# A decoder layer on one core: the down-projection summed over two pairs of weight blocks, five shared PSUM banks, weight tiles prepared one at a time

## What is computed

```python
x = x + mamba_and_mlp(layernorm(x))           # MLP: 2048 hidden columns, float32 weights
x = x + smooth_quant_experts(layernorm(x))    # one small expert for each of the 4 sequences
x = x + ffn(layernorm(x))                     # FFN: 4096 hidden columns, 4-bit weights
...
hn = _rmsnorm(h, rms2_w)                      # h: the residual after the Mamba block
mlp = jax.nn.silu(hn @ gate_w.T) * (hn @ up_w.T) @ down_w.T
return res + mlp
...
Wg = dequant_nvfp4(gate_W_packed, gate_scales)     # code -> value, times a scale per 32 columns
gate = jnp.einsum('th,nh->tn', xt, Wg)
up = jnp.einsum('th,nh->tn', xt, Wu)
gelu = jnp.tanh(0.7978845608028654 * (gate + 0.044715 * gate ** 3)) * gate * 0.5 + gate * 0.5
out = jnp.einsum('tn,hn->th', gelu * up, Wd)
```

## Time and profile before

| | |
|---|---|
| median of 3 runs | 3127.9 us (3126.78 to 3128.18) |
| the profiled execution | 3122.57 us, span of its instructions 3120.8 us |
| PE busy | 2763.6 us (89%) |
| DVE busy | 2285.1 us (73%) |
| ACT busy | 1158.0 us (37%) |
| POOL busy | 1099.5 us (35%) |
| weight stage (first gate matmul to last add) | 1268.5 to 3115.9 us |
| DMA | 275.37 MB, mean 88 GB/s |

### The profile page before, as it was taken

One profiled execution on the slowest core, in us unless ns is written; L12 is line 12 of the kernel. 1 busy time (PEld: TensorE's weight loads), 2 busy tenths in 40 slices (PEclk: granted clock), 3 DMA queues, 4 the chain that ended last, 5 costly groups with the idle time before them and its releaser, 6 DMA issues.

```text
span 3120.8 us, 32784 instructions
## 1 busy us (share of the span) xinstructions
PE 2763.6 (89%) x11248; PEld 1932.1 (62%) x11248; DVE 2285.1 (73%) x2903; ACT 1158.0 (37%) x1668; POOL 1099.5 (35%) x776
## 2 busy tenths in 40 slices
PE   6488898888888857999999999899999999999998
PEld 2344444444444235778777777777777777777777
DVE  6599999999999954444476667777776666676664
ACT  3355555555555433332244433332332321222221
POOL 0288888888888811010000001111111111212210
PEclk8798998888889668999999999999999999999999
DMA  3554555456455254011111012112111111111111
GB/s 131 179 171 143 161 150 155 142 158 163 130 171 145 58 212 155 21 68 61 61 41 59 23 41 61 41 41 61 39 39 37 29 56 46 42 41 41 42 55 59
DMA packets 152215, 275.37 MB, mean 88 GB/s; under 512 B 27248, under 2 KB 27760, under 8 KB 151536
## 3 DMA queue, kind: packets, MB, share of 16 engines
q1 hardware_dynamic: 152048, 273.27, 28.6%
HBM read 178.27 MB, written 61.34 MB: 77 GB/s over the span
## 4 chain that ended last, share of the span: by engine, by line
PE 47%; DVE 21%; ACT 10%; SPq 7%; issue 6%; POOL 6%; DMA 3%; DVEq 0%; POOLq 0%; ACTq 0%
PE ps L1508 11%; PE ps L1510 10%; PE ps L1509 10%; PE ps L1548 7%; ACT ps L764 4%; PE ps L1558 4%; DVE state L1165 4%; SPq L603 3%; POOL wdeq L1053 3%; DVE alo L1460 2%; PE ps L1620 2%; POOL read L1019 2%; DVE prod L1454 2%; DVE glo L1228 2%; SPq L607 1%
## 5 line engine op out<-in xcount | busy, mean ns | idle before, releaser
L1053 POOL TENSOR_TENSOR wdeq<-packed,scales 128x1024 f32<-128x1024 f16 x96 | 229.7, 2392 | 1454.4 <-DVE packed L1285 1020.9
L1019 POOL TENSOR_TENSOR read<-state,c_t 128x512 f32<-128x512 f32 x512 | 655.1, 1291 | 141.2 <-DVE state L1165 117.5
L1165 DVE TENSOR_TENSOR_SCAN state<-ps,drive 128x512 f32<-128x512 f32 x512 | 618.3, 1208 | 14.1 <-ACT ps L764 13.1
L1508 PE MATMUL ps<-xh,ghi 128*128 128x512 f32 x1536 | 609.1, 397 | 1.7 <-DVE res L1220 0.9
L1510 PE MATMUL ps<-xh,glo 128*128 128x512 f32 x1536 | 598.4, 390 | 0.0
L1509 PE MATMUL ps<-xl,ghi 128*128 128x512 f32 x1536 | 598.1, 389 | 0.0
L764 ACT ACTIVATE ps<-ps,a_exp 128x512 f32<-128x512 f32 x512 | 338.9, 662 | 468.2 <-PE ps L1548 467.2
L1508 PE MATMUL ps<-ahi,ghi 128*128 128x512 f32 x768 | 323.1, 421 | 93.3 <-DVE res L1439 74.8
L1439 DVE TENSOR_TENSOR res<-res,ps 128x512 f32<-128x512 f32 x384 | 258.7, 684 | 184.5 <-PE ps L1510 183.9
L1156 DVE TENSOR_TENSOR drive<-ps,b_t 128x512 f32<-128x512 f32 x512 | 339.8, 664 | 21.7 <-PE ps L1548 21.1
L1548 PE MATMUL ps<-dpack,sel 128*128 128x512 f32 x512 | 261.0, 510 | 103.9 <-DVE state L1165 102.3
(11 more groups left out here) (167 smaller groups left out, 3709.5 us busy)
## 6 DMA issues: line engine op xcount, KB each, us to landing
whi<-w_d SPq DMA_DIRECT2D x63, 256.0 KB, 3.9
wlo<-w_d SPq DMA_DIRECT2D x63, 256.0 KB, 4.8
x_d<-ev SPq DMA_DIRECT2D x32, 256.0 KB, 3.1
x_t<-x_d SPq DMA_DIRECT2D x32, 256.0 KB, 4.8
b_d<-ev SPq DMA_DIRECT2D x32, 256.0 KB
b_t<-b_d SPq DMA_DIRECT2D x32, 256.0 KB, 4.0
c_d<-ev SPq DMA_DIRECT2D x32, 256.0 KB, 3.0
c_t<-c_d SPq DMA_DIRECT2D x32, 256.0 KB, 3.2
```

The lines of the kernel that those rows point to most:

```text
L1019: pool.tensor_tensor(read[:, n % RRING, :], state[:, n % SRING, :], c_t[:, g % 2, :], ALU.mult).then_inc(read_ready, 1)
L1053: pool.tensor_tensor(wdeq[:, :].rearrange("p (h n) -> p h n", h=2), codes, scale, ALU.mult).then_inc(deq, 1)
L1165: dve.tensor_tensor_scan(state[:, n % SRING, :], ps[:, n % 2, :], drive[:, n % DRING, :], 0.0, ALU.mult, ALU.add)\
L1508: pe.matmul(out_, w_h, x_h, start=(start and k == 0), stop=False)
```

## The change

1. **Two passes become one, of 24 slots (index E).** Slots 0 to 15 make gate and up for eight units (two pairs), slots 16 to 23 make eight down products, one a slot, each summed in PSUM over both pairs: 12 matmuls instead of 6. There are 24 double passes with the same 6912 matmuls, and each residual block is added once in a double pass: 192 adds instead of 384. `ahi` and `alo` have four tiles each instead of two.
2. **Five shared banks.** Every product of the stage, gate, up or down, takes the next of banks 0 to 4 in turn. `bank_taken(V)` waits for the reader of the product five slots before.
3. **Weight tiles one by one.** There is a ring of five places for `ghi`/`glo`. Tile T (six for each double pass) is loaded at slot 4T - 19, unpacked at 4T - 14, its high part made at 4T - 12, its low part at 4T - 11. Raw data have two buffers, each for one tile, loaded by 1 DMA for the MLP, and by 9 for the FFN (1 for codes, 8 for scales), once tile T - 2 has been dequantised or split.
4. `prod` is gone: DVE multiplies in place into `act_o`, and ACT waits for `alo` of the unit before the last before it writes `act_o` again.
5. Ahead of the stage tiles 0 and 1 are prepared where three were, tile 2 five steps of the output projection later, tiles 3 and on inside the loop.

```diff
-    ghi = [[post(f"ghi{s}{w}", [P, 1024], F32R, R1 + 24576 * s + 4096 * w) for w in range(3)]
-           for s in range(2)]
...
-    prod = [post(f"prod{s}", [P, S], F32, R1 + 69632 + 2048 * s) for s in range(2)]
+    ghi = [post(f"ghi{s}", [P, 1024], F32R, R1 + 8192 * s) for s in range(WRING)]
...
+    ahi = [post(f"ahi{j}", [P, 2 * S], F32R, R1 + 40960 + 8192 * j) for j in range(4)]
...
+        def prepared_at(p, off):
+            T, rest = divmod(p + 12 - off, 4)
+            return [T] if rest == 0 and 3 <= T < ALL_T else []
+        def free_bank(V):
+            return V % 5
...
@@ SP @@
-                for w, name in enumerate(("gate", "up", "down")):
-                    sp.dma_start(packed[:, w, :], t[name + "_codes"][q]).then_inc(codes_loaded, 16)
+                if T >= MLP_T + 2:
+                    sp.wait_ge(deq, T - MLP_T - 1)
+                elif T >= 2:
+                    sp.wait_ge(w_lo, T - 1)
...
@@ ACT @@
-                if Q:
-                    act.wait_ge(gate_ready, 4 * (Q - 1) + 1)
+                if E and k == 0:
+                    act.wait_ge(up_ready, 8 * E - 4)
+                if E and k == 1:
+                    act.wait_ge(gate_ready, 8 * E)
+                if E and k == 2:
+                    act.wait_ge(up_ready, 8 * E)
...
+                if E and k in (3, 4):
+                    act.wait_ge(down_ready, 8 * E)
+                if k == 5:
+                    act.wait_ge(gate_ready, 8 * E + 4)
...
                     if U >= 2:
-                        act.wait_ge(prod_done, U - 1)
+                        act.wait_ge(a_lo, U - 1)
...
-                if i in (4, 6, 8) and Q + 1 < ALL_Q:
-                    w_high(Q + 1, i // 2 - 2)
+                for T in prepared_at(p, 0):
+                    w_high(T)
...
@@ DVE @@
-            for p in range(12 * ALL_Q + 1):
...
+            for p in range(24 * ALL_E + 1):
+                E, i = divmod(p, 24)
+                if i == 0 and E:
+                    add_down(E - 1, 7)
...
-                if i in (9, 10, 11):
-                    for k in (2 * i - 18, 2 * i - 17):
-                        add_down(8 * Q + k)
-                if i in (1, 3, 5) and MLP_Q <= Q + 1 < ALL_Q:
-                    unpack(Q + 1, i // 2)
-                if i in (5, 7, 9) and Q + 1 < ALL_Q:
-                    w_low(Q + 1, i // 2 - 2)
+                if i >= 17:
+                    add_down(E, i - 17)
+                for T in prepared_at(p, -2):
+                    if T >= MLP_T:
+                        unpack(T)
+                for T in prepared_at(p, 1):
+                    w_low(T)
...
@@ PE @@
-                        if f == 0:
-                            pe.wait_ge(a_lo, 4 * Q + 3 + bb)
-                        if D_ >= 2:
-                            pe.wait_ge(added, D_ - 1)
+            def bank_taken(V):
+                if V >= 5:
+                    E, i = divmod(V - 5, 24)
+                    if i >= 16:
+                        pe.wait_ge(added, 8 * E + i - 15)
+                    elif i % 2:
+                        pe.wait_ge(prod_done, 8 * E + i // 2 + 1)
+                    else:
+                        pe.wait_ge(act_done, 8 * E + i // 2 + 1)
+                return ps[:, free_bank(V), :]
...
+                    if i == 16:
+                        pe.wait_ge(w_lo, 6 * E + 6)
+                    if f == 0:
+                        pe.wait_ge(a_lo, 8 * E + 7 + bb)
+                    d = [((6 * E + 4 + j // 2) % WRING, D * (j % 2) + P * f) for j in range(4)]
+                    three_pass(bank_taken(p), [
+                        (ghi[s][:, at:at + P], glo[s][:, at:at + P],
+                         ahi[j][:, cols(bb)], alo[j][:, cols(bb)]) for j, (s, at) in enumerate(d)])\
+                        .then_inc(down_ready, 1)
```

More of the change, by code:

```diff
@@ L305, in build @@
         x_added = sem("x_added")
-        w_loaded4 = sem("w_loaded4")
-        codes_loaded = sem("codes_loaded")
+        tile_loaded = [sem(f"tile_loaded{s}") for s in range(2)]
         bits = sem("bits")
@@ L565, in load_chunk, with load_tile @@
                       .then_inc(yz_loaded[m % CHUNKS], 16)
[L567 to L572 removed]
+            def load_tile(T):
+                Q, w = tile_of(T)
+                ffn, h, q = stage(Q)
+                if T >= MLP_T + 2:
+                    sp.wait_ge(deq, T - MLP_T - 1)
+                elif T >= 2:
+                    sp.wait_ge(w_lo, T - 1)
+                if not ffn:
+                    sp.dma_start(graw[T % 2][:, :], t[("gate_w", "up_w", "down_w")[w]][q])\
+                      .then_inc(tile_loaded[T % 2], 16)
+                    return
+                sp.dma_start(packed[T % 2][:, :], t[("gate_codes", "up_codes", "down_codes")[w]][q])\
+                  .then_inc(tile_loaded[T % 2], 16)
+                for bl in range(8):
+                    rows = slice(16 * bl, 16 * bl + 16)
+                    if w < 2:
+                        sp.dma_start(scales[T % 2][rows, :].rearrange("p (k n) -> p k n", k=2),
+                                     t[("gate_scales", "up_scales")[w]][q, bl].unsqueeze(0)
+                                     .broadcast_to([16, 2, 256])).then_inc(tile_loaded[T % 2], 16)
+                    else:
+                        sp.dma_start(scales[T % 2][rows, :],
+                                     t["down_scales"][q, bl].unsqueeze(0).broadcast_to([16, 512]))\
+                          .then_inc(tile_loaded[T % 2], 16)
             def load_x_raw(b):
@@ L623, in load_w2 @@
                 sp.dma_start(w2[:, :, :], t["w2"][b]).then_inc(w2_loaded, 16)
-            for p in range(12 * ALL_Q):
-                Q, i = divmod(p, 12)
-                if i == 8 and Q + 2 < MLP_Q:
-                    load_mlp(Q + 2)
-                if i == 6 and MLP_Q <= Q + 2 < ALL_Q:
-                    load_ffn(Q + 2)
+            for p in range(24 * ALL_E):
+                for T in prepared_at(p, -7):
+                    if T >= 5:
+                        load_tile(T)
                 if p in (24, 36):
@@ L1457, in _ @@
+                if i % 2 == 1 and 3 <= i <= 17:
                     n = i // 2 - 1
-                    U = 4 * Q + n
+                    U = 8 * E + n
                     dve.wait_ge(a_hi, U + 1)
-                    dve.tensor_tensor(alo[n // 2][:, cols(n % 2)], prod[n % 2][:, :],
+                    dve.tensor_tensor(alo[n // 2][:, cols(n % 2)], act_o[n % 2][:, :],
                                       ahi[n // 2][:, cols(n % 2)].bitcast(F32), ALU.subtract)\
                        .then_inc(a_lo, 1)
-                if i in (9, 10, 11):
-                    for k in (2 * i - 18, 2 * i - 17):
-                        add_down(8 * Q + k)
```

222 lines of the change are left out of this document (101 added, 121 removed).

## The result

| | before | after |
|---|---|---|
| median, beside each other | 3127.34 us (3126.73 to 3128.18) | 3002.05 us (3001.17 to 3003.91) |
| ratio | | 0.960, 95% interval 0.9583 to 0.9617 |
| the profiled execution | 3122.57 us | 3002.58 us |
| weight stage, first gate matmul to last add | 1268.5 to 3115.9 us | 1268.6 to 2995.9 us |

The forecast was 3002.0.

A forecast was written before the change was run, and what follows sets the result against it. PE bounds the weight stage, losing time at down products; 141 us removable less 15 kept or new gives 126, so 3122.6 becomes 2997, plus 5.3 to the median: 3002 us. Forecast 2984 to 3018 (0.70); range 2982 to 3034.

The forecast's parts named there:

- What bounds the kernel: Weight stage: bound by PE, whose losses stand at down products, waiting for residual adds (74.8 us) and `alo`.
- Adds, 74.8 us: Down products: with five shared banks no add should stop PE any more, so 74.8 us in 42 waits go.
- DVE's wait for DMA goes too, without value for PE: First unpack of a pass: single-tile loads come in time, so DVE's wait for DMA goes, worth nothing to PE.
- 192 adds fewer: DVE in the weight stage: 131 us less work, off the path except through lag, no value of its own.
- `alo` at the heads, 9 us: First down products: the wait for `alo` stays, 24 times instead of 48; 9 us kept of 17.1.
- Background, 2 us: Background work on PE: it reaches its waits for ACT and DVE earlier, adding 2 us, at worst 12.
- Clock, 37 us lost with 4 left: Weight stage: half-speed clock after waits costs 37 us; with long waits at two or three places, 4 remain.
- The removable 141 us: Weight stage: waits for adds 74.8, `alo` waits 17.1, hidden parts 9, short waits 3 and clock 37 us.
- Port: Rival, chance 0.11: after slot 14's unpack POOL's dequantisation wins against `alo` each time, 0.9 us in 16 double passes; 3020 us.
- Queue: Rival, whole or half, chance 0.10: lag moves from down heads to PE's background waits for DVE and ACT; 3025 to 3072 us.
- Tiles late: Rival, chance 0.03: single-tile loads through two raw buffers outlast PE's pace; at a 25 us load 290 us slower, 3400.
- Adds still stop PE: Down products: adds would still stop PE only with a DVE lag over 10 us; counted with the queue rival.

The follow-up runs named there:

- the version with both edits: Changed kernel with background steps starting 3 (h = 0) and 6 (h = 1) slots later, and unpack and both splits of a tile one slot later: 2979.52 us.
- the unpack behind `alo`: Changed kernel with the unpack and both splits of a tile one slot later, so that `alo` comes first in a slot's work: 2988.34 us, ratio 0.956.

## Why the prediction was right, step by step

**What bounds the kernel: right.** Waits at down products went, the rest of PE's work stayed, and the stage is 120 us shorter. The starts of all matmuls of the stage in the two profiled executions say where the time went. Each gap between starts above 0.2267 us is counted once:

| us | forecast | measured |
|---|---|---|
| listed waits | 80.9 (74.8 + 17.1, less 9 and 2) | 71.4 (99.1 to 27.7) |
| matmuls 0.43 us apart in rows of three or more, the lower clock level | 33 (37 less 4) | 25.6 (142 of them to 14, 28.4 to 2.8) |
| hidden by the modelled ends, beside listed waits | 9 | 7.0 (8.0 to 1.0) |
| short pauses that are not listed | 3 | 4.9 (16.0 to 11.1) |
| slow start behind pauses, gaps of 0.23 to 0.38 | none | 10.1 (16.2 to 6.1) |
| around background products | none | 1.4 |
| sum | 126 | 120.4 |

**Adds, 74.8 us: right in size, incomplete in cause.** All 42 waits are gone. But there was a second cause that the prediction did not see: five banks alone remove these waits and give only 58 us, because DVE, set back by the late load, is then waited for at `alo` (55.8 us).

**"DVE's wait for DMA goes too, without value for PE": wrong.** It goes, in after and in the kernel with early loads. Loading tile by tile, which removes it, gives 36 us alone and 64 us on top of the banks (3069.6 to 3006.0). The step that failed was to read the DMA wait as idle time of an engine that does not bound. In before DVE stood up to 4.7 us at the start of a pass and had not caught it up when the adds and `alo` came for which PE waited: without that standing 42 waits for adds sum to 60.4 us instead of 74.8. The forecast came out all the same, because the change removes this cause too and the sum counted the waits wherever they came from.

**192 adds fewer, "no value of its own": wrong by 12 us.** 132 us of DVE put back cost 12.

**`alo` at the heads, 9 us: mis-sized, 17.2 in 6 waits.** The sum named four places by slot numbers, and all four waits are in the trace: at slot 112, 1.7 forecast and 1.83 measured (1593.22); at 208, 0.7 and 1.20 (1914.39); at 280, 2.1 and 9.38 (2143.47); at 352, 0.7 and 2.99 (2385.66). Two more, of 0.71 and 1.05 us, were not named. The large one is sequence 3 with t = 5 and 7. The sum counted DVE's own instructions. Left out were ACT's background steps with their table loads ahead of `act_o`, behind which DVE stands 3.35 and 2.20 us; what two heavy steps in a row add up to; and the meeting with POOL (3.56 instead of 1.66 us for the scaling).

**Background, 2 us: mis-sized.** Listed waits of this kind were 5.3 us in before and are 9.7: 4.4 more.

**Clock, 37 us lost with 4 left: somewhat too optimistic.** The mean of the stage was 0.98 and is 1.00 to the printed digit up to 2980. Behind the 9.38 us wait the first gap is 0.57 us and the next eleven 0.43. Matmuls in rows at that pace cost 28 us before and 3 after, so 26 came back. By the length of the stretches at the lower level, 78.5 us before and 17.1 after, at half speed, it would be 39 and 9, so 31. The second count takes in time in which PE stood anyway, as 2139.0 to 2143.4 in after, at 0.50 without a matmul. Both are under the 33 forecast.

**The removable 141 us: too small, and this made up for part of the terms above.** From profiled execution to profiled execution the version with both edits gains 142.4 us and still has 6.7 us of waits. What was under-sized was the pace: 0.230 a matmul was read from passes that were taken as undisturbed. The undisturbed pace is 0.2267, so these four passes lost 1.76 us, 0.44 each. Over the stage what comes with pauses beyond their listed length (hidden by the ends, not listed, slow start) gave 7.0, 4.9 and 10.1 us, 22.0 together, where the sum had 12.

**From the profiled execution to the median.** 3122.6 less 126 gave 2997; measured is 3002.6. The 5.3 us that were then added came from one pair of numbers of before. In after the profiled execution and the median are the same (3002.58 and 3002.05). So 5.6 us too much gain and 5.3 us of addition cancelled. The gain was right to 5%, but with errors of 9 and 7 us one way and 10 the other inside it; the last digit was chance.

**Rivals.** *Port*: fell. Where the two meet late in the FFN, `alo` begins first, keeps 0.68 us, and POOL pays. In means, `alo` first (after) gives 764 and 2709 ns, the dequantisation first (the unpack behind `alo`) 838 and 2396. The Trainium skill (SBUF — State Buffer, "Who interferes with whom") says that issue order decides who blocks; the trace agrees on both sides. *Queue*: right in kind, small in size. Lag moved to the background as 4.4 us. *Tiles late*: fell, with room: 25 DMAs a tile cost nothing that can be told from noise (3005.7 and 3002.1, intervals overlap). *Adds still stop PE*: fell. Of the terms put at nothing, the one ahead of the stage was right (it begins at 1268.6 for 1268.5); that of `act_o` in place was not run apart.

## What to carry to other kernels

An idle time of a helper engine costs nothing only if what it does next has slack. Take the waits one by one, and ask of each engine that is waited for whether it was late because of its own work or because of an earlier wait: two such causes hide each other, and cures tried alone look smaller than they are together (94 against 122 us here). Where engines run in order, the lateness of a result is the sum over all of them, table loads included; and the pace of the bounding engine has to be read where it has truly run undisturbed, since 0.230 for 0.2267, 1.5% off, hid 10 us here.

## What the runs showed of the hardware

- After a pause the matmul stream of before does not start at its pace, at a granted clock of 1.00. Behind the pause of 0.28 us that ends at 1403.84 the first gap is 0.34 us and the second 0.24. The next twelve take 2.76 us, 0.230 each, and the twelve after these 2.72, 0.2267 each:

```profile
1404.18 0.40 PE L1509 MATMUL ps<-alo,ghi 128*128 128x512 f32 x1
1404.42 0.40 PE L1510 MATMUL ps<-ahi,glo 128*128 128x512 f32 x1
...
1407.18 0.39 PE L1510 MATMUL ps<-ahi,glo 128*128 128x512 f32 x1
...
1409.90 0.39 PE L1510 MATMUL ps<-ahi,glo 128*128 128x512 f32 x1
```

- The meeting of DVE and POOL goes both ways in one kernel, and in these two cases the one that starts second loses about what the other had left: a dequantisation that began at 2122.70 beside the multiplication of 2.29 us (2122.53 to 2124.82) took 4.39 us against 2.4 alone; the scaling of `x_a` above is the other way round, 1.9 longer where POOL had 2.1 left.
- A table load of ACT took 1.28 us each time, and both background steps of ACT ahead of the 9.38 us wait brought two.
- SP needed 0.34 (8.09 / 24) to 0.46 us (3.67 / 8) for each DMA of scales that it issued. In before the first of 27 in a row was issued at 2711.69 and the last at 2723.90, 12.2 us later; DVE's unpack, which waits for all of them, began at 2725.82.
